# Sorting tokens by expert: rows written plainly, blocks collected by indexed DMAs, and the MLP's products in another order

## The reference

```python
def rms_norm(x, w):
    xf = x.astype(jnp.float32)
    var = jnp.mean(xf * xf, axis=-1, keepdims=True)
    return (w * (xf * jax.lax.rsqrt(var + EPS))).astype(x.dtype)

vm = expert_mask(token_type_ids)[..., None]     # one bit per token: which expert's weights
...
hidden_states = hidden_states + cctx @ cdense_w          # end of the two attentions
mi = rms_norm(hidden_states, ln_post_attn_w)
v_out = jax.nn.silu(mi @ v_gate) * (mi @ v_up) @ v_down  # 256 -> 688 -> 256
l_out = jax.nn.silu(mi @ l_gate) * (mi @ l_up) @ l_down
hidden_states = hidden_states + jnp.where(vm, v_out, l_out)
```

## Time and profile before

| what | value |
|---|---|
| median of three runs | 1456.5 us |
| the profiled execution | 1455.64 us |
| its span, first to last instruction | 1453.6 us |
| PE busy | 1293.3 us, 89% |
| DVE, ACT, POOL busy | 816.9, 762.6, 495.9 us |
| share of PE in the chain that ended last | 66% |
| phase 1's loop | about 165 to 470 us |
| from phase 1's end into the MLP loop | about 464 to 533 us |
| the MLP's loop and its last products | about 533 to 695 us |

### The profile page before, as it was taken

The page is one execution under the profiler, slowest core; times in us unless marked ns, Lnnn a source line. Parts: engine busy times, 40 slices in busy tenths (PEclk is TensorE's granted clock), DMA queues, the critical chain, the costliest instruction groups (busy, mean ns, idle before and its releaser), DMA issues.

```text
span 1453.6 us, 31426 instructions
## 1 busy us (share of the span) xinstructions
PE 1293.3 (89%) x10046; PEld 1041.9 (72%) x10047; DVE 816.9 (56%) x1739; ACT 762.6 (52%) x2905; POOL 495.9 (34%) x674
## 2 busy tenths in 40 slices
PE   6978689889889858888779999989989999998999
PEld 5754355455445447666668888879988888887999
DVE  3764365556456653333546655566664666566664
ACT  2324555565466563333566666574257666666432
POOL 2344665665566431112253233230011332332100
PEclk9999899999999779999889999999999999999999
DMA  6230000000000020001310000002001000000000
GB/s 231 79 113 25 5 12 1 12 11 4 8 11 11 8 112 30 29 29 30 90 30 5 5 4 7 0 1 96 0 0 63 5 5 4 4 4 1 9 22 29
DMA packets 21378, 41.58 MB, mean 29 GB/s; under 512 B 2928, under 2 KB 16368, under 8 KB 20592
## 3 DMA queue, kind: packets, MB, share of 16 engines
q1 hardware_dynamic: 18096, 34.01, 6.8%
q0 software_dynamic: 3200, 6.56, 1.8%
HBM read 34.01 MB, written 8.91 MB: 30 GB/s over the span
## 4 chain that ended last, share of the span: by engine, by line
PE 66%; POOL 9%; issue 8%; DVE 7%; ACT 5%; DMA 2%; SPq 1%; DVEq 0%; POOLq 0%; ACTq 0%
PE bank L1024 57%; PE bank L1037 9%; ACT p L1815 2%; DVE stats L1474 1%; POOL rstd L1994 1%; POOL xn L2009 1%; POOL p L2044 1%; POOL kv L2044 1%; DMA ctxT<-in_ctxT 1%; POOL x_all L2080 1%; DVE pT L1444 1%; DMA xn<-x_sorted 1%; DVE nmax L1562 1%; POOL o L2044 1%; POOL x_sorted L2071 1%
## 5 line engine op out<-in xcount | busy, mean ns | idle before, releaser
L1562 DVE TENSOR_REDUCE nmax<-bank 128x4 f32<-128x512 f32 x256 | 165.2, 683 | 138.8 <-PE bank L1024 138.2
L1815 ACT ACTIVATE p<-bank,nmax 128x128 f32<-128x128 f32 x512 | 180.5, 389 | 82.4 <-DVE nmax L1562 82.3
L1444 DVE COPY pT<-bank 128x512 f32<-128x512 f32 x256 | 165.0, 681 | 95.9 <-PE bank L1037 95.4
L2044 POOL TENSOR_TENSOR p<-p,rshare 128x512 f32<-128x512 f32 x128 | 132.1, 1052 | 219.5 <-DVE rshare L1569 219.4
L1024 PE MATMUL bank<-w_ff_rounded,hT_rounded 128*128 128x256 f32 x768 | 167.7, 286 | 4.2 <-ACT w_ff_rounded L1955 3.8
L1024 PE MATMUL bank<-kv,hT 64*128 64x128 f32 (+2 forms) x1280 | 148.6, 361 | 1.0 <-ACT p L1815 0.9
L1024 PEld LDWEIGHTS bank<-w_ff_rounded,hT_rounded 128*128 128x128 f32 x768 | 129.9, 194 | 5.4 <-issue 4.1
L1024 PE MATMUL bank<-pT,kv 128*32 128x128 f32 (+1 forms) x2048 | 117.0, 292 | 16.9 <-DVE pT L1444 7.2
L1024 PEld LDWEIGHTS bank<-pT,kv 128*32 128x32 f32 (+1 forms) x2048 | 82.0, 128 | 68.9 <-issue 35.2
L1815 ACT ACTIVATION_READ_ACCUMULATOR p<-bank,nmax 128x1 f32 x512 | 117.0, 228 | 0.0
L1024 PE MATMUL bank<-w_ff_rounded,o_rounded 128*128 128x256 f32 (+1 forms) x472 | 115.5, 290 | 0.6 <-issue 0.6
(11 more groups left out here) (213 smaller groups left out, 3334.5 us busy)
## 6 DMA issues: line engine op xcount, KB each, us to landing
ctxT<-in_ctxT SPq DMA_DIRECT2D x32, 128.0 KB, 2.4
w_att<-in_w2a SPq DMA_DIRECT2D x1, 3072.0 KB
w_att<-in_w3a SPq DMA_DIRECT2D x1, 3072.0 KB
w_ff<-in_w1b SPq DMA_DIRECT2D x4, 688.0 KB, 6.6
w_att<-in_w1a SPq DMA_DIRECT2D x1, 2304.0 KB
x_sorted<-in_x POOLq DMA_DIRECT2D x4, 576.0 KB, 11.5
xn<-x_sorted SPq DMA_DIRECT2D x18, 128.0 KB, 2.0
y_sorted<-o SPq DMA_DIRECT2D x18, 128.0 KB, 1.7
```

The source lines that it names most:

```text
L1444: dve.tensor_copy(dst, src).then_inc(sems[s[0], "copied"], 1)
L1562: dve.tensor_reduce(nmax[:, s[4], :], bank[:, :].rearrange("p (h t) -> p h t", h=QUAD), AX_X, ALU.max, negate=True).then_inc(sems[s[0], "m ...
L1815: t = act.activation(p[:, part], bank[:, part], ACT.Exp, bias=nmax[:, g, j:j + 1], accum_out=rsum[:, g, j:j + 1])
L2044: t = pool.tensor_tensor(p, p, rshare[:, g + n, :].unsqueeze(2).broadcast_to([P, QUAD, P]), ALU.mult)
```

## The change

Rows now go out in their own order, by plain DMAs of SP (`store_x`, two rows each, into `x_rows`), and the sorting is done on the way in: POOL's `load_block` collects 128 rows of a half by an indexed DMA from `x_rows`, with row numbers from a table `src`. The scatter steps, their copies and the four filling DMAs are gone. `index_rows` is now 16 operations on DVE at the same place of the program. They build two 0/1 tables (`lane_hot`, with 128x2048 elements, and `block_hot`), and a new step `place` turns them into `src` with 32 matmuls of nine columns on PE and a copy on DVE. `place` and the first loads stand in the table between phases 1 and 2. In the MLP loop, POOL issues the load of a unit's next block right after the reciprocal root of its present one, and the accumulating gathers of rows 0 to 7 from iterations 6 to 8 on, where they stood behind the loop. SP loads `w2a` and the two context tiles in iteration 1 of the MLP instead of ahead of it. And `steps_mlp1` has another order.

```diff
 def steps_mlp1(norms, pre):
     def part(u):
         v, of_v = (B_, here) if u == A_ else (A_, ahead)
-        return (of_v(("gu", v, 0)) + ahead(("norm_self", u)) + here(("hT", u, 0)) + of_v(("gu", v, 1))
-                + ahead(("scale_mlp", u)) + here(("hT", u, 1)) + ahead(("xT1", u)) + of_v(("gu", v, 2))
-                + here(("down", u)))
+        return (ahead(("norm_self", u)) + here(("hT", u, 0), ("hT", u, 1)) + of_v(("gu", v, 0), ("gu", v, 1))
+                + ahead(("scale_mlp", u)) + of_v(("gu", v, 2)) + ahead(("xT1", u)) + here(("down", u)))
...
-                ([], of_v(("cv", v), ("cq", v)) + keys_c[1:], here(("cdense", u, 1), ("end", u), ("scatter", u)))]
+                ([], of_v(("cv", v), ("cq", v)) + keys_c[1:], here(("cdense", u, 1), ("end", u)))]
...
 ORDER 2:
-        mix.self.1.0.0 scores_cross.cross.0.0.0 turn.self.1.0.2
+        place.0 load.0.0 mix.self.1.0.0 scores_cross.cross.0.0.0 turn.self.1.0.2
...
+            def store_x(it, u):
+                sp.wait_ge(*after(PHASES[1], it, ("end", u), "done"))
+                h, at = divmod(UNITS * ROWS * it + ROWS * u, HALF_ROWS)
+                sp.dma_start(x_rows[h][:, at:at + ROWS, :], x_all[:, rows(it, u), :]).then_inc(x_out[u], 16)
...
                     for it in range(ph.iters):
-                        if it + 1 < ph.iters:
-                            load_block(it + 1, B_)
-                        store_block(it, A_)
-                        if it + 2 < ph.iters:
-                            load_block(it + 2, A_)
-                        store_block(it, B_)
+                        for u in range(UNITS):
+                            store_block(it, u)
+                        if it == 1:
+                            sp.dma_start(w_att[:, 0:W2A_COLS], dram["w2a"]).then_inc(weights_att, 16)
...
+            def load_block(it, u):
+                k = UNITS * it + u
+                for w in range(UNITS):
+                    pool.wait_ge(x_out[w], STORES_OF_X * (k // BLOCKS + 1))
+                pool.wait_ge(*after(PHASES[2], 0, ("place", 0), "copied"))
+                if it == 0:
+                    pool.wait_ge(*after(PHASES[1], ITERS - 1, ("nT", u), "mm"))
                 else:
+                    pool.wait_ge(*after(PHASES[2], it - 1, ("xT1", u), "mm"))
+                pool.indirect_dma_start(x_block[u], None, x_rows[k // BLOCKS].rearrange("p b d -> (p b) d"),
+                                        bass.IndirectOffsetOnAxis(src[:, k:k + 1], 0)).then_inc(block_in[u], 16)
...
+            RETURNS = {(6, A_): (0, 1), (6, B_): (2, 3), (7, A_): (4,), (7, B_): (5,), (8, A_): (6,), (8, B_): (7,)}
+            def norm_block(ph, it, s, bank):
+                u = s[1]
+                to_rstd(ph, it, s, bank)
+                if ph.index != 2 or it == 0:
+                    return
+                if it + 1 < ph.iters:
+                    load_block(it + 1, u)
+                for row_at in RETURNS.get((it, u), ()):
+                    gather_row(row_at)
...
+                then(dve.tensor_tensor(lane_hot, to.unsqueeze(2).broadcast_to([P, B, P]),
+                                       lane.unsqueeze(1).broadcast_to([P, B, P]), ALU.is_equal))
```

More of the change, by code:

```diff
@@ L364 @@
     "cv": "mm copied", "coT": "copied", "cdense": "mm", "xT1": "mm hi lo", "gu": "mm silu product", "hT": "mm hi lo",
-    "scatter": "", "mrow": "done", "ctx2": "near lo hi", "half": "done", "nT2_low": "",
+    "place": "copied", "mrow": "done", "ctx2": "near lo hi", "half": "done", "nT2_low": "",
     "down": "mm copied", "q2": "mm copied", "k2": "mm copied", "v2": "mm copied", "oT2": "mm hi lo", "oT2_low": "",
@@ L411, in __init__ @@
                      for late, kind in enumerate(kinds) if 0 <= i - late < len(self.once)]
+        if index == 2:
+            self.once += [("place", 0)] + [("load", u, it) for it in range(2) for u in range(UNITS)]
+            self.place["place", 0], self.of_kind["place"], self.after["place"] = 0, 0, 1
         if index == 3:
-            self.once += [("gather", b) for b in range(B)]
+            self.once += [("gather", b) for b in range(HALF_ROWS, B)]
         jobs = [s for s, _ in body if "mm" in EVENTS[s[0]]]
@@ L490 @@
         split.experts.3 finish.experts.2 scores_cross.cross.1.0.3 cdense.0.1 round.experts.5 end.0
-        share_cross.cross.1.0.0 scatter.0 scores_cross.cross.1.1.0 split.experts.4 scores_cross.cross.1.1.1
+        share_cross.cross.1.0.0 scores_cross.cross.1.1.0 split.experts.4 scores_cross.cross.1.1.1
         share_cross.cross.1.0.2 turn_cross.cross.1.0.0 turn_cross.cross.1.0.1 finish.experts.3 norm_self.0
@@ L498 @@
         mix_cross.cross.1.1.0 finish.experts.8 split.experts.10 turn_cross.cross.1.1.2 turn_cross.cross.1.1.3
-        cdense.1.0 finish.experts.9 xT1.0 mix_cross.cross.1.1.1 half.1 finish.experts.10 coT.1.1 norm_self.1
-        gu.0.0 cdense.1.1 end.1 scatter.1 gu.0.1 scale_mlp.1 gu.0.2 xT1.1 round.experts.11 round.experts.12
+        cdense.1.0 finish.experts.9 xT1.0 load.0.1 mix_cross.cross.1.1.1 half.1 finish.experts.10 coT.1.1 norm_self.1
+        gu.0.0 cdense.1.1 end.1 gu.0.1 scale_mlp.1 gu.0.2 xT1.1 load.1.1 round.experts.11 round.experts.12
         split.experts.11 round.experts.13 split.experts.12 finish.experts.11 round.experts.14 split.experts.13
@@ L860, in run, with once @@
                     entered(ph)
[L861 removed]
+                def once(it):
                     for s, early in ph.body:
@@ L864, in run @@
                             stages[s[0]](ph, it + early, s, ps[ph.bank[s]] if s in ph.bank else None)
+                if ph.index in unrolled:
+                    for it in range(ph.iters - 1):
+                        once(it)
+                else:
+                    with eng.Fori(0, ph.iters - 1) as it:
+                        once(it)
             for p, it, s in between(None):
@@ L1733, in entered @@
                 dve.memset(every_row, 1.0).then_inc(setup_v, 1)
+                dve.memset(running[:, :, :, :], 0.0).then_inc(setup_v, 1)
+                n = VECTOR_SETUP - 6
+                upper = slice(HALF_ROWS, 2 * HALF_ROWS)
+                dve.wait_ge(setup_v, n)
+                dve.tensor_copy(running[:, 0, :, upper], vm[:, :, 0].rearrange("p (h b) -> p h b", h=HALVES)).then_inc(setup_v, 1)
+                for i in range(3):
+                    old, new = i % 2, 1 - i % 2
+                    dve.wait_ge(setup_v, n + i + 1)
+                    dve.tensor_tensor(running[:, new, :, upper], running[:, old, :, upper],
+                                      running[:, old, :, HALF_ROWS - 2 ** i:2 * HALF_ROWS - 2 ** i], ALU.add).then_inc(setup_v, 1)
             def ready(ph):
@@ L2122, in _ @@
+            stages = dict(load=load, gather=gather, share=share, share_cross=share, mrow=media_rows, spread_self=spread_self, spread_cross=spread_cross, out0=to_rstd, norm_self=norm_block,
                           norm_cross=to_rstd, scale_self=scale_self, norm_ln=to_rstd, qk=qk)
```

209 lines of the change are left out of this document (102 added, 107 removed).

## The result

The changed kernel takes 1387.38 us (median of four runs, 1382.78 to 1388.48) where the kernel before took 1455.44 on the same chip: a ratio of 0.9526, 95% interval 0.9492 to 0.956. The forecast was 1395.2, 7.8 us too long. That is close, but partly because errors of both signs cancel, as the stages show. Each boundary is the start of the same PE instruction in both traces ("the w_att product" is the last one with `w_att` ahead of phase 1's loop), and the profiled execution's span went from 1453.6 to 1385.4 us.

A forecast was written before the change was run, and what follows sets the result against it. PE, busy 1293.3 of 1453.6 us, was taken as the bound. Gains of 28.3 (MLP), 27.5 (scatters), 2.5 (index arithmetic), 0 (place) and 3 (start) summed to 61.3 us: 1395.2 from the median, range 1378 to 1422.

The forecast's parts named there:

- MLP order: MLP loop: the new step order removes PE's 1.6 us wait for xn in 15 halves, 24.0 us gained.
- a sign against the forecast: MLP loop: PE standing before the first gu matmul by "issue" or a register load would show the forecast wrong.
- rival 1: MLP loop: the register load is uncovered in every block, or a similar stall appears; 9.5 us less gain, 1405; chance 0.15.
- Scatters gone: Phase 1's loop: 4.1 us wait plus 1.4 us slow work saved per half, 27.5 us; bounds 20.5 and 33.
- Rival 2: Phase 1: something else is late next, so only 2 us per half is won; 17.5 us less, 1413; chance 0.16.
- a wait that I cancelled against `place`: Behind phase 1's loop: the 1.91 us wait for POOL's o set against 2.2 us for place; zero, -3 to +3.
- Index arithmetic: Phase 1's loop entry: about 6 us on DVE replaces PE's 9.31 us wait; 2.5 us gained, bounds 0 and 5.
- Rival 5: Place and the index arithmetic cost double, 7 us each, not 2.2 and 6; 8 us less, 1403; chance 0.06.
- First block: MLP's first pass: PE's 7.91 us wait shrinks to 1.5 us for DVE's chain, 6.4 us gained.
- the 1.5 us that I charged for them: MLP: loads cost nothing themselves, but iteration 6's gathers delay the other unit's root; 1.5 us lost in all.
- Rival 3: MLP: indexed loads are on the path once issue to landing exceeds 12.1 us; chance 0.03 in part, 0.02 in full.
- rival 4: POOL is held about 2.5 us longer issuing indexed DMAs beside a busy DVE; 11 us less, 1406; chance 0.06.

The follow-up runs named there:

- scale_early: The changed kernel with the MLP's scale_mlp step one place earlier, between the other block's first and second thirds; 1372.26 us.
- xn_thrice: The changed kernel with POOL computing xn three times in each half of phase 1's loop and at its entry, no scatters; 1434.06 us.
- w2a_first: The changed kernel with the w2a load and the two context loads back ahead of the MLP in SP's queue; 1385.1 us.
- pool_held: The changed kernel with POOL's kv product at phase 1's loop entry waiting until DVE's index arithmetic is done; 1382.17 us.
- fills_back: The changed kernel with four 576 KB DMAs issued from POOL at the start again, into a tensor nobody reads; 1392.11 us.
- xn_twice: The changed kernel with POOL computing xn twice in each half of phase 1's loop and at its entry; 1415.57 us.

## Why the forecast was near, and where it was wrong

**MLP order: right that the wait goes, wrong that nothing takes its place.** Forecast 24.0 for 15 halves at 1.6. From the first block's xn transposes to the last down but one, PE went from 148.46 us to 132.36 (492.97 to 625.33), 16.1 us less: sixteen halves at 1.0. I had looked at the register load ahead of gu and called it covered by a whole down before the change. That was misread: the earlier trace rows have 0.49 and 0.51 us by "issue" ahead of the first gu product, so PE standing there, which I had named as a sign against the forecast, is nothing new. The load ahead of down I had not looked at, though PE's order in the change has xT1 directly ahead of down. It took 9.8 us, near the 9.5 that stood as the bound. scale_early shows it: with the scaling earlier, the issue waits go from 12.9 to 1.5 us and a half takes 7.0. The Trainium skill ("DMA: Bandwidth & Descriptors", section "Latency and other measured facts") puts such a load at 600 ns at least; the gaps of 0.58 to 0.72 us ahead of down agree in size, and by that sentence rival 1 deserved more than 0.15.

**Scatters gone: the term was right, the clock's part too small.** The wait gave back 4.1 us per half as worked out, but the slow stretch 2.9, not 1.4. I had priced only the two pieces that I listed, 1.83 us together, and taken less than both. One row for the whole stretch, 6.7 us at 0.52, gives 3.2. That is 7.0 per half, 34.1 in all, a little over my upper bound of 33. xn_thrice shows wait and clock as cause. Rival 2 is out: PE's next largest wait in that loop is 2.4 us in six pieces.

**Behind the loop: a wait that I cancelled against `place` had a tail.** `place` cost 0.96 us and a wait of 1.15, 2.1 together; 2.2 was forecast. But the wait of 1.91 us had a slow stretch behind it, 472.9 to 486 us at a granted clock of 0.61, and after the change it is gone. Measured from marker to marker, the kernel after gained another 3.2 us by the end of the last half, lost 2.1 to `place`, and won about 6.3 in that stretch: most of the 8.7. The clock of PE in the two stretches, before and after:

```profile
472.90:486.00 13.10, 13.07 (x48) 6.09 (x48) 6.53 (x12) 8.03 (x42) 4.29 (x5) 0.61 0.00 1
419.00:440.00 21.00, 18.47 (x181) 9.82 (x180) 14.35 (x29) 15.97 (x84) 12.09 (x13) 1.00 0.06 20
```

No run isolates these; they are read from the two timelines, and the gain is not the same in every execution. In w2a_first, whose edit does nothing before 487 us, the same wait of 1.15 us ahead of `place` is followed by 17 us at 0.70, and the stretch from `place` to the MLP takes 3.2 us longer.

**Index arithmetic: 9.1 us, not 6.** The sum was right, 6.05 us with POOL idle in pool_held; what it left out was POOL beside it. pool_held shows that POOL's products stopped three of these DVE operations, each with two inputs in SBUF. The Trainium skill ("SBUF — State Buffer", section "Who interferes with whom") says just this of a DVE instruction with two SBUF inputs beside a GpSimd instruction that reads SBUF; the rows agree (0.90, 0.96 and 1.90 us beside POOL, 0.17, 0.17 and 0.33 without). In xn_thrice a cast with one input was stopped as well. Rival 5 came true in part, 9.1 us here but 2.1 for `place`; its price of 8 us does not follow from its own figures, which give (7 - 2.2) + (7 - 6) = 5.8.

**First block, loads, start.** The first block's wait fell by 5.0 us instead of 6.4, since the weight splits on DVE are the last to end; up to the xn transposes the gain is 3.4. The indexed loads cost nothing, and the 1.5 us that I charged for them were not lost in the kernel after, only with the tighter order of scale_early. Rival 3 is out (5.6 us at most against the 12.1 at which it begins), and so is rival 4: loads were issued in 1.02 to 1.22 us beside a busy DVE. The start gave 6.4 us, more than the wait of 3.9: the kernel before ran at 0.83 from 20 to 30 us, and fills_back brings wait and low clock back together.

So the slow work behind waits was under-priced by some 7 us in phase 1, the stretch behind the loop by 9 (6 of them one wait with its slow stretch), and the start by 3; the MLP, with its new stall and the smaller gain at the first block, gave 8.8 less than forecast, and the entry 3.4 less.

## What to carry to other kernels

Price a wait of PE with the slow stretch behind it, read as one window's granted clock and not from the first two pieces: here 4.1 us of wait were 7.0. Where the last producer ahead of a register load is moved close to it, look at every such load on the path, and ask which instruction of another engine sets that producer's start. When small operations move to DVE, look at what POOL does beside them; here the same arithmetic cost 9 us at one place and under 4 at three others.

## What was not expected of the hardware

- Waits of PE of about the same length left the granted clock at 1.00 one time (2.76 us) and at 0.70 over the next 17 us four times (2.42 to 2.76 us), all in one trace. The wait of 1.15 us ahead of `place` left it at 1.00 in the kernel after and at 0.62 to 0.70 in xn_thrice, xn_twice and w2a_first. Waits of 4.2 to 4.8 us brought 0.50 to 0.53 over the next 6.7 us each time. This stays open.
- A DVE operation on 128x16 elements took 0.90 to 1.89 us beside a POOL product and 0.12 to 0.17 without.
- Three megabytes on another queue stretched the longest landing of an indexed load only from 5.6 to 9.0 us.
